# Selective scans of two bidirectional Mamba layers: every third input product on GpSimd with its decay in PSUM, B and C rows spread by DMA from a DRAM copy, units of both channel halves

## The reference, cut to what matters

```python
def selective_scan(u, dt, A, Bm, Cm, Dskip):
    dA = jnp.exp(dt[..., None] * A)
    dBu = (dt * u)[..., None] * Bm[:, :, None, :]

    def step(h, inp):
        dA_t, dBu_t, C_t = inp
        h = dA_t * h + dBu_t
        return (h, jnp.einsum('bdn,bn->bd', h, C_t))
    ...
    return jnp.moveaxis(ys, 0, 1) + u * Dskip

def _one_dir(x, cw, cb, xpw, dpw, dpb, A_log, Dskip):
    xc = jax.nn.silu(causal_conv1d(x, cw, cb))
    proj = xc @ xpw.T
    dt_r, Bm, Cm = jnp.split(proj, [DT_RANK, DT_RANK + D_STATE], axis=-1)
    dt = jax.nn.softplus(dt_r @ dpw.T + dpb)
    A = -jnp.exp(A_log)
    return selective_scan(xc, dt, A, Bm, Cm, Dskip)
```

## Time and profile before

| | |
|---|---|
| time, median of 3 runs | 3814.8 us (3814.68 to 3815.76) |
| profiled execution | 3814.13 us, its span 3812.4 us |
| busy share of the span | PE 73%, DVE 77%, ACT 45%, POOL 37% |
| TensorE clock granted, mean | 0.895 |
| one scan block, forward | first scan at 178.2 us, last at 399.6 us |
| one scan block, backward | first scan at 468.3 us, last at 696.6 us |

### The profile page before, as it was taken

How to read it: one execution, slowest core, us unless ns; L and a number is a source line. 1 busy time by engine, 2 the same in 40 slices (tenths; PEclk the granted TensorE clock), 3 DMA queues, 4 the chain that set the end, 5 groups by cost and what they waited for, 6 DMA issues and landing times. The chain is left out here.

```text
span 3812.4 us, 36609 instructions
## 1 busy us (share of the span) xinstructions
...
## 2 busy tenths in 40 slices
...
DMA packets 39359, 67.81 MB, mean 18 GB/s; under 512 B 8512, under 2 KB 26896, under 8 KB 39024
## 3 DMA queue, kind: packets, MB, share of 16 engines
...
q0 software_dynamic: 512, 1.05, 0.1%
...
...
## 5 line engine op out<-in xcount | busy, mean ns | idle before, releaser
L515 DVE TENSOR_TENSOR m1x_HS<-m1x_HF,m1x_HS 128x512 fp32r<-128x512 f32 x256 | 260.1, 1016 | 0.2
L509 DVE TENSOR_TENSOR m1x_HF<-m1x_R,m1x_pg 128x512 f32<-128x512 f32 x256 | 176.1, 688 | 56.2 <-ACT m1x_R L485 23.2
L485 ACT ACTIVATE m1x_R<-m1x_ph,m1s_BX 128x512 f32<-128x512 f32 x256 | 176.4, 689 | 80.8 <-PE m1x_ph L309 79.2
L1873 POOL TENSOR_TENSOR t0x1bs_HC<-t0x1bs_HS,t0x1bs_CB 128x1024 f32<-128x1024 f32 x64 | 150.7, 2355 | 126.7 <-DVE t0x1bs_HS L1863 126.7
L1873 POOL TENSOR_TENSOR t0x0bs_HC<-t0x0bs_HS,t0x0bs_CB 128x1024 f32<-128x1024 f32 x64 | 150.7, 2355 | 126.5 <-DVE t0x0bs_HS L1863 125.1
L1873 POOL TENSOR_TENSOR t0x1fs_HC<-t0x1fs_HS,t0x1fs_CB 128x1024 f32<-128x1024 f32 x64 | 150.6, 2354 | 121.2 <-DVE t0x1fs_HS L1863 121.2
L1873 POOL TENSOR_TENSOR t0x0fs_HC<-t0x0fs_HS,t0x0fs_CB 128x1024 f32<-128x1024 f32 x64 | 150.6, 2353 | 119.5 <-DVE t0x0fs_HS L1863 117.6
L492 ACT ACTIVATE m1x_HS<-m1x_HF 128x512 fp32r<-128x512 f32 x256 | 159.9, 624 | 65.0 <-DVE m1x_HF L509 65.0
L333 POOL TENSOR_TENSOR m1s_WR<-m1s_W,m1s_ZERO 128x1024 fp32r<-128x1024 f32 x32 | 77.0, 2408 | 302.3 <-PE m1x_acc L309 302.1
L683 ACT ACTIVATE m0x_S<-m0x_pa 128x512 f32<-128x512 f32 x128 | 76.6, 598 | 176.3 <-PE m0x_pa L309 176.3
L307 PE MATMUL m1x_acc<-m1x_HS,m1s_WR 128*128 128x512 f32 x256 | 109.4, 427 | 61.5 <-DVE m1x_HS L515 61.5
...
## 6 DMA issues: line engine op xcount, KB each, us to landing
...
out<-g_H SPq DMA_DIRECT2D x1, 1024.0 KB, 3.9
...
```

Source lines behind the costliest of these rows:

```text
L485: nc.scalar.activation(R[:, k % 2, :], ph[k % 4][:, :], ACT.Relu, bias=BJ[:, j, c:c + 1]).then_inc(relu_ready, 1)
L509: nc.vector.tensor_tensor(HF[:, k % 2, :], R[:, k % 2, :], pg[(k // C) % 2][:, :], ALU.mult).then_inc(gated, 1)
L515: nc.vector.tensor_tensor(HS[:, k % 4, 1, :], HF[:, k % 2, :], HS[:, k % 4, 0, :].bitcast(F32), ALU.subtract).then_inc(low_made, 1)
L1873: nc.gpsimd.tensor_tensor(HC[:, m % 2, :], HS[:, m % 2, :], CB[:, m % 2, :], ALU.mult).then_inc(hc_made, 1)
```

## The change

1. **Units.** A unit is now one state, both channel halves and 512 tokens, again 128 x 1024. The selector matmul of B runs once for each half with the same operands, and the exponential needs two instructions (one scale for each half), each of 128 x 496.
2. **Every third unit's product on POOL** (`by_pool`: m % 3 == 2). POOL's `feed(m)` multiplies `DU` by the row of B in `BB` into `DB` (SBUF). For these units the decay goes to `pd` (PSUM), and DVE scans `pd` and `DB` with no product before it. The other 43 units of a block keep the product on DVE in `pb`.
3. **B and C rows by DMA.** The first block copies the 96 rows with ACT to `BCF` (SBUF), DVE splits from there, and SP stores 32 rows (256 KB) to the DRAM tensor `bc_rows`. In the scan block SP loads C for four units at a time, spread to 128 partitions (1 MB, `load_c`, 16 for a block), and B for each POOL unit (256 KB, `load_b`, 21 for a block), two buffers each. `spread_c`, `pc` and `copy_c` are gone, and `spread_b` is left out for POOL's units.
4. **Depth.** `HS` has four buffers and `HC` three. The waits on earlier units are looser by one or two, and `read_sum` stands behind the decay of unit 16k+3 instead of 16k+1.

The diff, cut to its core:

```diff
@@ mamba_direction, first block
+        bc_rows = nc.dram_tensor(name + "_bc_rows", (2 * DS, T), F32, kind="Internal").ap()
...
+                    sp.wait_ge(rows_read, GROUPS)
+                    sp.dma_start(bc_rows[:, :], BCF[0:2 * DS, :]).then_inc(rows_stored, 16)
+                    sp.wait_ge(rows_stored, 16)
...
-                        dve.wait_ge(bcd_made, g + 1)
-                        split(nc, link, parts, pp[0][0:96, g, :], BC[:, g * GROUP:(g + 1) * GROUP])
-                        dve.sem_inc(bc_read, 1)
+                        dve.wait_ge(rows_read, g + 1)
+                        split(nc, link, parts, BCF[:, g * GROUP:(g + 1) * GROUP], BC[:, g * GROUP:(g + 1) * GROUP])
...
+                        a.activation(BCF[:, g * GROUP:(g + 1) * GROUP], pp[0][0:96, g, :], ACT.Copy).then_inc(rows_read, 1)
@@ mamba_direction, scan block
+                    def load_c(j):
+                        if j >= 2:
+                            sp.wait_ge(hc_made, CN * (j - 1))
+                        m = CN * j
+                        rows = bc_rows[N + m % N:N + m % N + CN, tokens(m)]
+                        sp.dma_start(CB[:, j % 2, :, :], rows.partition_broadcast(P)).then_inc(cb_loaded[j % 2], 16)
+                    def load_b(k):
+                        if k >= 2:
+                            sp.wait_ge(db_made, k - 1)
+                        m = 3 * k + 2
+                        sp.dma_start(BB[:, k % 2, :],
+                                     bc_rows[m % N, tokens(m)].partition_broadcast(P)).then_inc(bb_loaded[k % 2], 16)
+                    loads = [(3 * k - 7, load_b, k) for k in range(UNITS // 3)]
+                    loads += [(CN * (j - 1), load_c, j) for j in range(UNITS // CN)]
+                    for _, load, i in sorted(loads, key=lambda x: x[0]):
+                        load(i)
...
-                        if m >= 2:
-                            pe.wait_ge(scanned, m - 1)
+                        if m >= 3:
+                            pe.wait_ge(scanned, m - 2)
...
-                        if m + 2 < UNITS:
+                        if m + 2 < UNITS and not by_pool(m + 2):
                             spread_b(m + 2)
-                            spread_c(m + 2)
                         add_up(m)
...
+                        out = pd if by_pool(m) else DA[:, m % 3]
+                        for dh in range(2):
+                            i = a.activation(by_sequence(out[:, dh, :])[:, :, rest],
+                                             by_sequence(DT[:, dh, tokens(m)])[:, :, rest], ACT.Exp,
+                                             scale=AN[:, dh, m % N:m % N + 1])
...
-                        if m > N and m % N == 1:
-                            read_sum(m - 2)
+                        if m > N and m % N == 3:
+                            read_sum(m - 4)
...
+                        if by_pool(m):
+                            dve.wait_ge(db_made, m // 3 + 1)
+                            decay, fed = pd, DB
+                        else:
+                            dve.wait_ge(b_made, on_dve(m) + 1)
+                            decay, fed = DA[:, m % 3], pb[m % 3]
+                            v.tensor_tensor(fed[:, :, :], DU[:, :, tokens(m)], fed[:, :, :], ALU.mult).then_inc(multiplied, 1)
+                            dve.wait_ge(multiplied, on_dve(m) + 1)
                         dve.wait_ge(da_made, m + 1)
-                        if m >= 2:
-                            dve.wait_ge(hc_made, m - 1)
+                        if m >= 4:
+                            dve.wait_ge(hc_made, m - 3)
...
+                    def feed(m):
+                        k = m // 3
+                        pool.wait_ge(bb_loaded[k % 2], 16 * (k // 2 + 1))
+                        if k:
+                            pool.wait_ge(scanned, m - 2)
+                        rows = BB[:, k % 2, :].unsqueeze(1).broadcast_to([P, 2, GROUP])
+                        nc.gpsimd.tensor_tensor(DB[:, :, :], DU[:, :, tokens(m)], rows, ALU.mult).then_inc(db_made, 1)
+                    feed(2)
                     for m in range(UNITS):
-                        pool.wait_ge(c_copied, m + 1)
+                        j = m // CN
+                        pool.wait_ge(cb_loaded[j % 2], 16 * (j // 2 + 1))
                         pool.wait_ge(scanned, m + 1)
-                        if m >= 2:
-                            pool.wait_ge(summed, m - 1)
+                        if m >= 3:
+                            pool.wait_ge(summed, m - 2)
...
+                        if by_pool(m) and m + 3 < UNITS:
+                            feed(m + 3)
```

More of the change, by code:

```diff
@@ L1757, in mamba_direction, with tokens, by_pool, on_dve @@
             rest = slice(0, L - 1) if back else slice(1, L)
-            def unit(m):
-                return m // (2 * N), m // N % 2, m % N
-            def tokens(th, g):
-                return slice(th * HALF + g * GROUP, th * HALF + (g + 1) * GROUP)
-            def columns(g):
-                return slice(g * GROUP, (g + 1) * GROUP)
-            with nc.Block() as block:
+            def tokens(m):
+                return slice(m // N * GROUP, (m // N + 1) * GROUP)
+            def by_pool(m):
+                return m % 3 == 2
+            def on_dve(m):
+                return 2 * (m // 3) + m % 3
+            with nc.Block() as block:
+                @block.sync
+                def _(sp):
+                    def load_c(j):
[14 more added lines that the diff above has]
+                        load(i)
                 @block.tensor
```

88 lines of the change are left out of this document (35 added, 53 removed).

## The result

The changed kernel takes 3839.9 us (median of 4 runs, 3835.8 to 3841.9) against 3815.1 us for the kernel before on the same chip: a ratio of 1.0063, with a 95% interval of 1.0046 to 1.0081. It is slower, by some 25 us. The forecast was 3804 us and the range ended at 3819. Among the runs further on, one execution of the kernel e6_sbuf_decay took 5674.1 us, 1.4 times its four others; it is left out, and its cause is not known.

The account below looks back on a forecast made before the run. DVE set the old pace; POOL would become the bound by little. Scan blocks -64 us and first blocks +0.5 give -63; lost clock +52 makes -11 against 3814.1: 3804 us, range 3748 to 3819.

Parts of the forecast that it names:

- The work of each engine: Scan blocks, three units: POOL 9.41 us at 2.353 a product, DVE 9.08, so POOL becomes the bound by little.
- The loads: Rival, scan blocks: DMA loads of B and C become the bound; at 90 GB/s 3860 us; chance 0.03.
- The start: Start of each scan block: POOL's first `HC` comes 6.5 us after the first instruction, before it was 5.0.
- The clock: PE rests 2.7 us behind POOL's product; 10 of 21 rests a block lose the clock, 1.3 us each, 52 us in all.
- The sum without clock: Four scan blocks save 64 us, first blocks lose 0.5: 3752 us; as the rival where the clock holds, chance 0.18.
- lost nearly every time: Rival, PE's rests behind POOL's product: clock lost in all 21 a block gives 3861 us; chance 0.07 (or for longer).
- decision point: Clock losses in a scan block at which the gain is used up: 63 / (4 x 1.3) = 12.
- The rule of the Trainium skill: PE's clock: the skill warns only of idle gaps longer than 2.7 us; by it the clock holds, 3752 us.
- new sums: Three places in each scan block: POOL waits 2.3 us forward and 4.1 us backward at each.
- the chain `HC`, `add_up`, spread, product, scan: From the end of `HC(m)` through `HC(m+3)` with hand-overs: 8.6 us against a period of 9.4.

Follow-up runs that it names:

- e6_sbuf_decay: The changed kernel with the decay of POOL's units written to SBUF (third buffer of `DA`) instead of PSUM: 3933.9 us.
- e8: The changed kernel with B spread three units ahead, before additions; first C load in four, first row early; B spread before a new sum's opening matmuls: 3705.4 us.
- e4_first_c: The changed kernel with its first load of C cut into four, the first row right behind the first row of B: 3810.3 us.
- e1_fill: The changed kernel with six bf16 matmuls of zeros ahead of `add_up` in units that follow POOL's product, except at new sums: 3779.8 us.

## Why the prediction was wrong, point by point

Two terms of the sum failed: the price of the start, and the number of times that the clock is lost. Both were in the sum, with sizes too small; together they turned a small gain into a loss.

**The work of each engine: right.** POOL's products take 2346 and 2382 ns (2353 taken), scans 2266 and 2287 ns, the first blocks nothing. POOL is the bound by its work; e8 shows the period of 9.27 us. The loads were no bound in the body of the changed kernel.

**The start: mis-sized.** It was priced by one broadcast load's 263 GB/s and a store's 3.9 us: 6.5 us. It is 11.4 us, at under 140 GB/s. The row it came from the earlier trace rows was of another load, over 1.2 us in its middle, and the start needs the time until a whole first load lands, two smaller ones ahead of it and the next ones issued before it has landed. The step also took the start as a plain shift of 1.5 us; it is PE's longest rest as well. Undone in most part, it gave back 29.6 us.

**The clock: right in mechanism, too low in size.** The place (PE's rest behind POOL's product), the way (`add_up` at the low clock) and the windows at 0.80 to 0.90 came as described. Losses were put at "about half" of 21 for a block, from one rest that lost the clock and one that didn't; it is some 16 in the forward block. The two rests were no equals either: the one from 117.00 us went on for 5.73 us, with the clock's fall some 2.2 us into it, the other ended after 2.47. The fillers put their cost at 60 us, against 52 in the sum: more losses, each a bit cheaper (14.2 / 16 = 0.9 us instead of 1.3).

**The two account for the miss.** The sum without clock was 3752. e4_first_c got 29.6 us for a start of 5.9 us; for the 6.5 us of the sum that is some 2 less (4 x 0.6), 27. With it the sum is 3779, and e1_fill, where the clock's loss is filled and the late start is left, took 3779.8. With e1_fill's 60 for the clock it is 3839, and the changed kernel took 3839.9. The sum had 52 for the clock. So of the 36 us of the miss some 27 are the start and 8 the clock. That the start's price contains what follows it is from e4_first_c; that these are two separate sums is an approximation, since both pass through the same chain. That it closes to 1 us is luck, for inside e1_fill the sum is wrong in places that about cancel: POOL's products come 2.32 us apart (three in 6.96) and not 2.38, some 21 us less over the four blocks, while its `HC` wait 50 us for scans (10.9, 16.5, 10.4 and 12.3) and not the 38 that the sum has for new sums. What the new sums alone cost the changed kernel no run isolates.

**The rival "lost nearly every time".** It had the right sign and mechanism, with a chance of 0.07. Its decision point, 12 losses for a block, was passed. The low chance was the error of judgement: the forecast's own 10 stood two losses from the point where the sign turns, and the range closed at 3819 though 109 us was named as the clock's upper end.

**The rule of the Trainium skill.** The prediction set "TensorE: Matmul & The Clock Gate", section "HAM oscillation — how this bites in real kernels", against the trace, by which a rest of 2.7 us would be harmless. Here rests of 2.25 to 2.44 us stand ahead of slow matmuls time and again, though others of 2.67 were harmless. The same page has, in "A second HAM failure mode: psum-queue depth-cycling", that many short rests between groups of matmuls can make the clock go up and down as well. The trace agrees that the clock can go up and down with rests this short; it does not agree that short rests are enough, for the kernel before rests in every unit, 0.54 us in the one shown, at a clock of 0.99.

**What was not seen at all.** The prediction checked that the chain `HC`, `add_up`, spread, product, scan has slack (8.6 of 9.4 us) at the full clock, and then charged it with the clock's loss. It did not ask why the spread should stand behind `add_up`. That order costs more than the clock: taking it away gave 108 us, filling the rests alone 60.
